# Expert tiles of 128 tokens, two per step with weights of their own, in an attention and mixture-of-experts kernel

## The chip, the cores and the metric

The kernel runs on one core of one Trainium2 chip. The metric is the device time of one execution in microseconds (us). A core has five engines with instruction streams of their own: TensorE (PE in the profile, its weight loads PEld), VectorE (DVE), ScalarE (ACT), GpSimd (POOL) and SyncE (SP), which here only issues DMAs. They meet by semaphores.

## The reference

```python
x = layernorm(x + attention(x))          # x: 8 x 512 x 256, float32
x = layernorm(x + experts(x))
# attention: 16 heads of 16, linear: q = elu(x Wq + bq) + 1, k likewise,
#   out = (sigmoid(x Wg + bg) * (q (k^T v))) Wo + bo
# experts: 16, inner width 128; softmax gate, 2 of 4 groups, top 4 of 16
a = silu(x w1[e]) * (x w3[e])
y = sum over the 4 chosen e of c[e] * (a w2[e])
z = silu(x ws1) * (x ws3) @ ws2          # shared expert, inner width 256
return y + z
```

## The kernel before

A float32 product is made of three half-width ones: each operand is split into a high part (float16, `_hi`) and a rest (bfloat16, `_lo`), and `product` (L1147) multiplies hi by hi, hi by lo and lo by hi. All expert weights lie in SBUF in both parts (`we_hi`, `we_lo`, 18 chunks: 2 of the shared expert, 16 of the others).

Stage one: a loop over 8 batches of 512 tokens does the attention, the first layer norm, and the routing. `assign_slots` gives each token a row in the region of each of its 4 experts, and GpSimd scatters the rows by indirect DMAs into `expert_in` in DRAM (`dispatch`). The batches are in two waves of 4 (2048 tokens, 8192 rows). SyncE meanwhile writes zeros into the rows behind the regions (`fill_spare`, 16 DMAs of 512 KB) and behind each region's last row (`fill_end`, 256 KB each, 16 for each wave; the second wave's 16 are issued one per step between steps 24 and 40 of the first wave).

Between the stages VectorE makes the plan of the first wave, `plan_pairs` in 8 dependent parts, which ends in two small tables on one partition: `pair_chunk` (the expert of each pair) and `pair_row` (its first row). Its place in VectorE's stream is behind `apply_gate(NB - 1)` and ahead of `shared_hidden(0)` and `residual(NB - 1)`. The shared expert of batches 0 to 2 is worked there too.

Stage two, the experts' steps: 48 steps for each wave, 96 in all. A step is a pair of 128-row tiles, 256 rows of one expert: 8192 rows are 32 pairs and each of the 16 experts may leave one begun. For each step
- SyncE reads the row number from `pair_row` into a register (L327), waits until the ring buffer of 4 is free, issues one load of 256 KB (L330), and waits for and issues the store of an earlier result (L334);
- TensorE's sequencer transposes the rows of step g + 2 (4 float32 transposes, L1340), reads the expert of step g from `pair_chunk` into a register (`chunk_of`, L1345), does `up_pair` (4 calls of `product`, 12 matmuls of 256 columns, with the expert's weights as the stationary operand, L1149 to L1151), then `down_pair` of step g - 2 (6 matmuls, L1367 to L1373). The steps stand in a loop over 8 of them; the first two of each turn of the loop read the expert of step g - 2 once more;
- ScalarE and VectorE split the transposed rows (L617, L1025), do silu (L634), the product with the other half (L1036), its split (L642, L1044), and the copy of the result (L624).

VectorE also has one small part of a plan or a weight table in each step of the first wave, and in the second wave it adds the first wave's gathered results (`combine`, L1055) and normalizes batches that are done (`final_norm`, L1070). GpSimd scatters the second wave's rows during the first wave's steps and gathers the first wave's results during the second's, both paced by `h_ready`, which `up_pair` counts up. Behind the last step the shared expert of the later batches and the gathering of the second wave remain.

The order on every engine is written out by hand.

```python
            def chunk_of(g):
                return pe.value_load(pair_chunk[0:1, g, :], min_val=SHARED, max_val=NCH - 1)
```

## Time and profile before

| | us |
|---|---|
| median of 3 runs | 711.87 (711.7 to 711.9) |
| the profiled execution | 707.36 |
| its span, first to last instruction | 705.5 |
| of it, attention stage | 0 to 230 |
| between the stages | 230 to 270.5 |
| the 96 steps | 270.5 to 589 |
| behind the last step | 589 to 705.5 |

The profile is one execution. Time stands in us from the span's start, durations of single instructions in ns where it is said. PE's matmuls are pipelined, so a matmul's duration is longer than the distance to the next one; the distance between starts is what a matmul costs in a stream. A "q" behind an engine's name marks instructions that its sequencer does alone: register operations, loads of a register from SBUF (TENSOR_LOAD), waits and the issue of DMAs. They don't count as busy time of the engine. The weight loads and matmuls are issued by one sequencer, and its own instructions are listed under PEldq.

### The profile page before, as it was taken

The numbers are of one execution on the slowest core, as the hardware profiler recorded it, in microseconds if no ns is written. First come the engines' busy times: TensorE is split into PE (matmuls) and PEld (weight loads), VectorE is DVE, ScalarE is ACT, GpSimd is POOL, SyncE is SP. The second block draws the span as 40 slices with busy tenths as digits, with TensorE's granted clock in tenths as the row PEclk, the third lists the DMA queues.
The fourth block names the chain that finished last, engine by engine and source line by source line (L and its number), as shares of the span: only waits on it lengthen the run. The fifth ranks groups of instructions, "written<-read, shape, count | busy, mean of one in ns | idle before, by whom it ended". The sixth has DMA issues, their size and how long they took to land.

```text
span 705.5 us, 13461 instructions
## 1 busy us (share of the span) xinstructions
PE 527.1 (75%) x3532; PEld 357.0 (51%) x3555; DVE 427.4 (61%) x1200; ACT 300.1 (43%) x659; POOL 290.1 (41%) x334
## 2 busy tenths in 40 slices
PE   1899887889897688789786688798888779665400
PEld 1355443555544357567574566576667566421300
DVE  2447783776864866666554444377757556652784
ACT  2536653436524343555454555356546445110100
POOL 1000126456446402454444200644446251777574
PEclk9999997899999899999999999899999989977755
DMA  7022428295451303767767766687787753333332
GB/s 202 13 75 76 156 90 284 82 304 209 177 185 68 103 18 106 239 204 230 232 228 259 238 223 216 180 235 233 211 261 231 223 181 134 105 120 89 94 114 99
DMA packets 64091, 118.63 MB, mean 168 GB/s; under 512 B 9760, under 2 KB 23088, under 8 KB 64048
## 3 DMA queue, kind: packets, MB, share of 16 engines
q1 hardware_dynamic: 51216, 84.55, 37.1%
q0 software_dynamic: 12288, 33.57, 15.1%
q8 instruction: 19, 0.31, 0.2%
q14 instruction: 24, 0.20, 0.1%
q10 hardware_dynamic: 544, 0.00, 0.0%
HBM read 55.17 MB, written 62.91 MB: 167 GB/s over the span
## 4 chain that ended last, share of the span: by engine, by line
PE 36%; DVE 19%; issue 15%; SPq 9%; another core or an unknown queue 6%; ACT 6%; DMA 5%; POOL 4%; ACTq 0%; DVEq 0%; POOLq 0%
PE t L1340 4%; PE h_even L1149 4%; PE h_even L1151 4%; PE h_odd L1149 3%; PE h_even L1150 3%; PE h_odd L1151 3%; PE h_odd L1150 3%; DVE x_all L1055 2%; SPq L327 2%; PE y L1186 2%; DMA kv<-expert_in 2%; SPq L330 1%; PE y L1373 1%; SPq L334 1%
## 5 line engine op out<-in xcount | busy, mean ns | idle before, releaser
L440 POOL DMA_INDIRECT expert_in<-x_all,slots x128 | 132.9, 1038 | 117.8 <-PE h_odd L1151 45.0
L452 POOL DMA_INDIRECT wa_stage<-expert_out,result_of x64 | 62.9, 983 | 35.3 <-issue 18.1
L1340 PE MATMUL t<-ident,kv 128*128 128x128 f32 x384 | 60.3, 280 | 19.4 <-DMA kv<-expert_in 15.0
L452 POOL DMA_INDIRECT q_fm<-expert_out,result_of x32 | 32.4, 1014 | 85.6 <-DMA expert_out<-q_exp 63.9
L426 POOL TENSOR_SCALAR neg_mean<-mv 128x4 f32<-128x4 f32 x16 | 4.6, 290 | 149.5 <-DVE mv L699 149.3
L1044 DVE TENSOR_TENSOR wa_lo<-bias_heads,wa_hi 128x256 bf16<-128x256 f32 x96 | 40.5, 422 | 41.3 <-ACT wa_hi L642 30.1
L1149 PE MATMUL h_even<-xsT_hi,we_hi 128*128 128x256 f16 x192 | 54.3, 283 | 10.7 <-issue 8.8
L1340 PEld LDWEIGHTS t<-ident,kv 128*128 128x128 f32 x384 | 45.3, 145 | 26.8 <-DMA kv<-expert_in 12.1
L1025 DVE TENSOR_TENSOR xsT_lo<-t,xsT_hi 128x512 bf16<-128x512 f32 x72 | 49.5, 688 | 11.6 <-ACT xsT_hi L617 5.9
L1150 PE MATMUL h_even<-xsT_lo,we_hi 128*128 128x256 bf16 x192 | 54.2, 282 | 2.5 <-issue 2.5
L1151 PE MATMUL h_even<-xsT_hi,we_lo 128*128 128x256 f16 x192 | 54.2, 282 | 1.4 <-issue 1.4
L617 ACT ACTIVATE xsT_hi<-t 128x512 f16<-128x512 f32 x72 | 42.0, 585 | 16.6 <-PE t L1340 12.8
L642 ACT ACTIVATE wa_hi<-bias_heads 128x256 f16<-128x256 f32 x96 | 39.7, 414 | 20.7 <-DVE bias_heads L1036 14.4
L1036 DVE TENSOR_TENSOR bias_heads<-h_odd,kv_heads 128x256 f32<-128x256 f32 x48 | 20.2, 420 | 41.8 <-ACT kv_heads L634 40.9
L1036 DVE TENSOR_TENSOR bias_heads<-h_even,kv_heads 128x256 f32<-128x256 f32 x48 | 20.1, 419 | 34.4 <-ACT kv_heads L634 30.9
L634 ACT ACTIVATE kv_heads<-h_odd 128x256 f32<-128x256 f32 x48 | 18.3, 381 | 52.8 <-remote 25.0
L1186 PE MATMUL y<-wo_sb,gated 128*128 128x256 f32 x128 | 33.3, 419 | 9.3 <-DVE gated L686 9.3
L452 POOL DMA_INDIRECT gate<-expert_out,result_of x32 | 30.5, 954 | 19.4 <-PE h_even L1151 10.0
L529 ACT ACTIVATE kv<-h_even 128x256 f32<-128x256 f32 x32 | 12.3, 386 | 58.3 <-PE h_even L1151 52.4
L634 ACT ACTIVATE kv_heads<-h_even 128x256 f32<-128x256 f32 x48 | 18.2, 380 | 43.8 <-PE h_even L1151 17.4
L1367 PE MATMUL y<-we_hi,wa_hi 128*128 x96 | 26.8, 279 | 12.6 <-issue 10.7
L624 ACT ACTIVATE k_exp<-y 128x512 f32<-128x512 f32 x48 | 28.7, 598 | 15.9 <-PE y L1373 14.3
(222 smaller groups left out, 1530.0 us busy)
## 6 DMA issues: line engine op xcount, KB each, us to landing
kv<-expert_in SPq DMA_DIRECT2D x96, 256.0 KB
expert_out<-k_exp SPq DMA_DIRECT2D x48, 256.0 KB
expert_out<-q_exp SPq DMA_DIRECT2D x48, 256.0 KB
expert_in<-wa_stage SPq DMA_DIRECT2D x16, 512.0 KB
expert_in<-wa_stage SPq DMA_DIRECT2D x32, 256.0 KB
stage<-in_L_ffn_w SPq DMA_DIRECT2D x48, 128.0 KB
x_in<-in_L_attn_x SPq DMA_DIRECT2D x8, 512.0 KB
out<-gated SPq DMA_DIRECT2D x8, 512.0 KB
```

Source lines behind the costliest of these rows:

```text
L440: pool.indirect_dma_start(xs_dram[b // WB], bass.IndirectOffsetOnAxis(ap=slots[:, b, t, j:j + 1], axis=0), x_all[:, b, t, :], None).then_i ...
L452: pool.indirect_dma_start(y_got[i][:, j, :], None, ys_dram[w], bass.IndirectOffsetOnAxis(ap=result_of[:, b, t, j:j + 1], axis=0)).then_inc ...
L617: act.activation(xsT_hi[r][:, :, :], t_bank[r % 2][:, :].rearrange("p (c n) -> p c n", c=KC), ACT.Copy).then_inc(xst_hi_ready, 1)
L642: act.activation(aT_hi[r % 2][:, :], a_pair, ACT.Copy).then_inc(at_hi_ready, 1)
L1025: dve.tensor_tensor(xsT_lo[r][:, :, :], t_bank[r % 2][:, :].rearrange("p (c n) -> p c n", c=KC), xsT_hi[r][:, :, :], ALU.subtract).then_in ...
L1036: dve.tensor_tensor(a_pair, h_banks[r % 2][0][:, 2 * P:], s_pair, ALU.mult).then_inc(pair_a_ready, 1)
L1044: dve.tensor_tensor(aT_lo[r % 2][:, :], a_pair, aT_hi[r % 2][:, :], ALU.subtract).then_inc(at_lo_ready, 1)
L1149: pe.matmul(dst, sta_hi, mov_hi, start=start, stop=False)
L1150: pe.matmul(dst, sta_hi, mov_lo, start=False, stop=False)
L1151: return pe.matmul(dst, sta_lo, mov_hi, start=False, stop=stop)
L1186: last = pe.matmul(y_bank[h][:, (t % 2) * D:(t % 2 + 1) * D], gated[:, c, t * P:(t + 1) * P], wo_sb[:, c, :], start=c == 0, stop=c == KC - 1)
L1340: last = pe.transpose(t_bank[r % 2][:, c * 2 * P + i * P:c * 2 * P + (i + 1) * P], xs[r][:, i, c * P:(c + 1) * P], ident[:, :])
```

## The change

The unit becomes a tile of 128 rows of one expert, planned tile by tile: 64 full tiles and 16 that may be begun give 80 tiles for each wave. A step takes two tiles, number g and number g + 40, and so two experts: 40 steps for each wave, 80 in all. Each step now reads two row numbers and issues two loads (of 128 KB, into 64 partitions each) on SyncE, reads two experts on TensorE, and does `up_pair` as 8 calls of `product` with 128 columns each. The transposes write every other column, so that the rows of each tile stand together. `down_pair` has 6 matmuls as before, with two experts' weights as the moving operand.

With it go: a ninth part in the plan, which works on 80 tiles where it worked on 48 pairs; a fifth part in `place_results`; half of the zero rows (8 DMAs of 512 KB, and 128 KB for each region's end); the pace of GpSimd's scatters and gathers in terms of the new steps; the final norm of batches 0 to 2 moved from VectorE to ScalarE (`final_norm` there), with a wait of GpSimd for it; the loops over the second wave's steps on VectorE and ScalarE written out. The plan of the first wave stands in VectorE's stream behind `residual(NB - 1)` and ahead of `shared_hidden(1)`. `gw_sb` shares the memory of `k_exp`, and several small tables that of `stage`.

```diff
-PLAN_STEPS = 8
+PLAN_STEPS = 9
...
-    NPAIR = WT * TOP_K // 2 + E
+    NTILE = WT * TOP_K + E
+    NPAIR = NTILE // 2
     PAIR = 2 * P
-    MOST = WB * S // PAIR
-    REGION = (MOST + 1) * PAIR
-    SPARE = NPAIR - WT * TOP_K // 2
-    SLOTS = E * REGION + SPARE * PAIR
+    MOST = WT
+    REGION = (MOST + 1) * P
+    SPARE = NTILE - WT * TOP_K
+    SLOTS = E * REGION + SPARE * P
...
-    PLAN_GROUPS = 7
+    PLAN_GROUPS = 8
+    NORM_PAIR = 17
...
-    assert SPARE * PAIR == FILLS * FILL_ROWS and FILLS == 8
+    assert SPARE * P == FILLS * FILL_ROWS and FILLS == 4
...
             def rows_of(dram, row):
-                return dram[bass.ds(row, PAIR), :].rearrange("(p t) d -> p t d", p=P)
+                return dram[bass.ds(row, P), :].rearrange("(p t) d -> p t d", t=2)
...
-                for i in range(4 * (b - 2), 4 * (b - 1)):
+                for i in range(3 * (b - 2), min(3 * (b - 1), WAVES * FILLS)):
                     fill_spare(i)
...
             next_x(NB - 1)
-            for i in range(12, WAVES * FILLS):
-                fill_spare(i)
...
             def load_xs(w, p, r, first=False):
 
-                row = sp.value_load(pair_row[0:1, NPAIR * w + p, :], min_val=0, max_val=SLOTS - PAIR)
+                rows = [sp.value_load(tile_row[0:1, h, NPAIR * w + p, :], min_val=0, max_val=SLOTS - P) for h in range(2)]
                 if not first:
                     sp.wait_ge(xs_transposed, NPAIR * w + p - RING + 1)
-                sp.dma_start(xs[r][:, :, :], rows_of(xs_dram[w], row)).then_inc(xs_loaded[r], 16)
+                for h in range(2):
+                    sp.dma_start(xs[r][h * P // 2:(h + 1) * P // 2, :, :],
+                                 rows_of(xs_dram[w], rows[h])).then_inc(xs_loaded[r], 16)
...
                 if 0 < k < WT:
-                    pool.wait_ge(h_ready, NPAIR + (3 * k if k < WT - TT else 3 * WT - 13 + 2 * (k - WT + TT)))
+                    pool.wait_ge(h_ready, NPAIR + 9 * k // 4)
...
                 if i > 0:
-                    pool.wait_ge(h_ready, 5 * i // 2)
+                    pool.wait_ge(h_ready, 2 * i)
...
-                        if b > 0 and t == (1 if w == 0 else TT - 1):
+                        if b > 0 and t == (2 if w == 0 else TT - 1):
+                            if 1 < b <= EARLY + 1:
+                                pool.wait_ge(out_ready, b - 1)
                             rstd_of(NB + b - 1)
...
+            for p in range(NPAIR):
+                pair(NPAIR + p, p % RING, GROUPS_OF_PAIRS + p // RING, p < NPAIR - 2)
+                b, t = (p - NORM_PAIR) // 9, (p - NORM_PAIR) % 9
+                if 0 <= b < EARLY and t < TT:
+                    final_norm(b, t)
...
             apply_gate(NB - 1, True)
-            for part in range(PLAN_STEPS):
-                plan_pairs(0, part)
...
             shared_hidden(0)
             residual(NB - 1, True)
+            for part in range(PLAN_STEPS):
+                plan_tiles(0, part)
             shared_hidden(1)
...
-                pe.wait_ge(xs_loaded[r], 16 * use)
+                pe.wait_ge(xs_loaded[r], 32 * use)
                 for c in range(KC):
+                    turned = t_bank[r % 2][:, c * PAIR:(c + 1) * PAIR].rearrange("p (k t) -> p k t", t=2)
                     for i in range(2):
-                        last = pe.transpose(t_bank[r % 2][:, c * 2 * P + i * P:c * 2 * P + (i + 1) * P],
-                                            xs[r][:, i, c * P:(c + 1) * P], ident[:, :])
+                        last = pe.transpose(turned[:, :, i], xs[r][:, i, c * P:(c + 1) * P], ident[:, :])
...
-            def chunk_of(g):
-                return pe.value_load(pair_chunk[0:1, g, :], min_val=SHARED, max_val=NCH - 1)
-
-            def up_pair(g, r, chunk):
+            def chunks_of(g):
+                return [pe.value_load(tile_chunk[0:1, h, g, :], min_val=SHARED, max_val=NCH - 1) for h in range(2)]
+
+            def up_pair(g, r, chunks):
...
-                for k in range(2):
-                    for c in range(KC):
-                        cols = slice((c * 2 + k) * INTER, (c * 2 + k + 1) * INTER)
-                        last = product(h_banks[r % 2][0][:, k * PAIR:(k + 1) * PAIR],
-                                       we_hi[:, chunk, cols], we_lo[:, chunk, cols],
-                                       xsT_hi[r][:, c, :], xsT_lo[r][:, c, :], c == 0, c == KC - 1)
+                for h, chunk in enumerate(chunks):
+                    tok = slice(h * P, (h + 1) * P)
+                    for k in range(2):
+                        for c in range(KC):
+                            cols = slice((c * 2 + k) * INTER, (c * 2 + k + 1) * INTER)
+                            last = product(h_banks[r % 2][0][:, k * PAIR + h * P:k * PAIR + (h + 1) * P],
+                                           we_hi[:, chunk, cols], we_lo[:, chunk, cols],
+                                           xsT_hi[r][:, c, tok], xsT_lo[r][:, c, tok], c == 0, c == KC - 1)
...
-                w2_hi, w2_lo = we_hi[:, chunk, W13:], we_lo[:, chunk, W13:]
...
+                for h, chunk in enumerate(chunks):
+                    last = product(y_bank[r % 2][:, h * D:(h + 1) * D],
+                                   aT_hi[r % 2][:, h * P:(h + 1) * P], aT_lo[r % 2][:, h * P:(h + 1) * P],
+                                   we_hi[:, chunk, W13:], we_lo[:, chunk, W13:], True, True)
```

## Rows read from the trace of the kernel before

**Rows 1.** Part 1 of the page: busy us, share of the span, instructions.

```profile
PE 527.1 (75%) x3532; PEld 357.0 (51%) x3555; DVE 427.4 (61%) x1200; ACT 300.1 (43%) x659; POOL 290.1 (41%) x334
```

**Rows 2.** Busy time by stretch: PE, PEld, DVE, ACT, POOL, clock, DMA share, GB/s.

```profile
270.50:589.00 318.50, 259.76 (x2089) 205.90 (x2090) 187.28 (x468) 165.16 (x378) 127.34 (x136) 0.96 0.69 219
...
370.00:390.00 20.00, 13.66 (x112) 10.38 (x110) 8.75 (x18) 8.99 (x21) 8.16 (x8) 1.00 0.78 254
...
110.00:120.00 10.00, 7.90 (x54) 3.61 (x54) 1.05 (x3) 2.73 (x4) 6.76 (x7) 0.99 1.01 366
```

**Rows 3.** Line 1149, 268 to 590: ns min/median/max, first to last start.

```profile
L1149 PE MATMUL h_even<-xsT_hi,we_hi x192: 269/273/421, 270.6 to 585.9; 128*128 128x256 f16 x192
...
L1149 PE MATMUL h_odd<-wa_hi,we_hi x96: 272/273/421, 277.8 to 587.8; 128*128 128x256 f16 x96
```

**Rows 4.** Timeline of PE, a step at full pace: start, us, instruction.

```profile
467.27 0.28 PE L1149 MATMUL h_even<-xsT_hi,we_hi 128*128 128x256 f16 x1
467.38 0.27 PE L1150 MATMUL h_even<-xsT_lo,we_hi 128*128 128x256 bf16 x1
...
469.68 0.27 PE L1149 MATMUL h_odd<-wa_hi,we_hi 128*128 128x256 f16 x1
```

**Rows 5.** TensorE's sequencer in one step, 469.45 to 471.78, by line.

```profile
L1149 PEldq FUSED_REGOPS  x4: 46/46/46, 469.5 to 470.2; - x4
...
L1151 PEldq ALU_OP  x4: 32/32/32, 469.6 to 470.3; - x4
...
L1364 PEldq EVENT_SEMAPHORE  x1: 51/51/51, 470.4 to 470.4; - x1
...
L1345 PEldq FUSED_REGOPS  x2: 42/96/151, 471.0 to 471.5; - x2
L1345 PEldq TENSOR_LOAD <-pair_chunk x1: 306/306/306, 471.1 to 471.1; - x1
L1345 PEldq SEQ_ASSERT  x1: 18/18/18, 471.7 to 471.7; - x1
```

**Rows 6.** The same view of line 1345 over all steps.

```profile
L1345 PEldq TENSOR_LOAD <-pair_chunk x118: 10/311/1293, 269.6 to 585.1; - x118
```

**Rows 7.** Timeline of weight loads, a step that begins on an idle PE.

```profile
388.69 0.10 PEld L1151 LDWEIGHTS h_even<-xsT_hi,we_lo 128*128 x1
388.84 0.10 PEld L1149 LDWEIGHTS h_even<-xsT_hi,we_hi 128*128 x1
```

**Rows 8.** Timeline of PE: matmuls of 32 columns, each with a weight load.

```profile
251.16 0.18 PE L1211 MATMUL t<-gwT_both,xT_hi 128*128 128x32 f16 x1
...
251.21 0.18 PE L1211 MATMUL t<-gwT_both,xT_hi 128*128 128x32 f16 x1
```

**Rows 9.** Waits of PE, 270 to 590: us in total, times, longest.

```profile
PE t L1340 <- DMA kv<-expert_in: 15.0, 11, 3.8
```

**Rows 10.** Timeline of weight loads in a starved stretch.

```profile
450.80 0.10 PEld L1369 LDWEIGHTS y<-we_lo,wa_hi 128*128 128x128 f16 x1 [0.61 <-issue]
```

**Rows 11.** Timeline of PE behind that stretch.

```profile
453.67 0.42 PE L1149 MATMUL h_even<-xsT_hi,we_hi 128*128 128x256 f16 x1
453.88 0.42 PE L1150 MATMUL h_even<-xsT_lo,we_hi 128*128 128x256 bf16 x1
```

**Rows 12.** SyncE's loads between 360.1 and 422: count, first to last issue.

```profile
L330 SPq DMA_DIRECT2D kv<-expert_in x17: 3/359/615, 360.9 to 421.4; - x17
```

**Rows 13.** All waits of SyncE in that stretch.

```profile
SPq L371 <- DMA expert_in<-wa_stage: 1.2, 1, 1.2
```

**Rows 14.** Timeline of DVE, the plan and the last residual.

```profile
232.15 0.99 DVE L844 TENSOR_TENSOR stage<-plan_sb,pairs_end 1x768 f32<-1x768 f32 x1
...
238.18 1.28 DVE L718 TENSOR_TENSOR x_all<-y,x_all 128x512 f32<-128x512 f32 x2
```

**Rows 15.** Timeline of ACT: the last batch's first norm.

```profile
243.37 2.07 ACT L510 ACTIVATE x_all<-x_all,shift,rstd 128x256 f32<-128x256 f32 x4 [0.82 <-POOL shift L431]
```

**Rows 16.** Timeline of SyncE: four fills of the attention stage.

```profile
108.05 3.12 SPq L292 DMA_DIRECT2D expert_in<-wa_stage  x4
```

More of the change, by code:

```diff
@@ L364, in _ @@
             sp.wait_ge(fill_rows_ready, 2)
[L365 to L367 removed]
+            with sp.Fori(2, (last - 1) // 2) as q2:
+                group(0, 2 * q2 + 1, fill=E + 2 * RING * (q2 - 2))
+                group(0, 2 * q2 + 2, fill=E + 2 * RING * (q2 - 2) + RING)
             sp.wait_ge(rows_ready, 2)
@@ L1026, in xst_lo, with pair @@
                                   xsT_hi[r][:, :, :], ALU.subtract).then_inc(xst_lo_ready, 1)
-            def pair(g, r, ahead=True, add=None, norm=None, whole=True, part=None):
+            def pair(g, r, ahead=True, add=(), part=None):
                 if ahead:
@@ L1037, in pair @@
                 if add:
-                    combine(0, *add[0], whole)
-                if norm is not None:
-                    final_norm(norm, r)
+                    combine(0, *add[0], add[0][0] < EARLY)
                 if part:
@@ L1073, in final_norm, with group @@
                     last.then_inc(out_ready, 1)
-            def group(q, b=None, tiles=(), norm=None, whole=True, parts=(), last=False):
+            def group(q, parts=()):
                 for r in range(RING):
-                    add = [(b, i // TOP_K, i % TOP_K) for i in tiles[r]] if tiles else None
-                    pair(RING * q + r, r, not (last and r >= 2), add, norm, whole,
-                         parts[r] if r < len(parts) else None)
-            q1 = GROUPS_OF_PAIRS
+                    pair(RING * q + r, r, part=parts[r] if r < len(parts) else None)
             xst_lo(0, 0)
```

151 lines of the change are left out of this document (74 added, 77 removed).

## The prediction

> **What bounds the kernel now.** I began with the page's first part [rows 1]: PE is busy for three quarters of the span, more than any other engine, but its busy time counts overlapping matmuls and is no proof of a bound. The busy times by stretch [rows 2] put 318.5 of the 705.5 us into the experts' steps, with the TensorE clock at 0.96, PE at 260 us, VectorE at 187 and ScalarE at 165. The change alters this stage most, so the rest is read there. The first and the last matmuls of line 1149 [rows 3] stand 317 us apart, so a step takes 317 / 95.5 = 3.32 us on average. The timeline of PE shows what a step costs when nothing is late [rows 4]: matmuls of 256 columns start 0.11 us apart, and the next step's first matmul starts 469.68 - 467.27 = 2.41 us later. Between them lie 12 matmuls of `up_pair`, 6 of `down_pair` and 4 transposes, 22 x 0.11. Of 3.32 us, then, 0.91 are stalls.
>
> The reader should next look at TensorE's sequencer, which no busy time shows. One step of it stands in [rows 5]. The four address computations of line 1149 run from 469.5 to 470.2 and the next wait (L1364) is at 470.4: about 0.95 us for `up_pair`, or 0.24 us for each `product` (one FUSED_REGOPS for the high weights' address, one ALU_OP for the low ones', six instructions for the array). `down_pair` and the transposes follow until 471.0: 0.55 us. Reading the expert into a register takes from 471.0 to the end of the view, where the next `up_pair` begins: 0.8 us (register operation, TENSOR_LOAD 0.31, register operation 0.15, assert, and the gaps between them). Together 2.3 us, just under the array's 2.41. The sequencer is hidden today by 0.1 us a step. That this rate is its own and not the array's is seen where a step begins on an idle PE [rows 7]: the first weight load behind an address computation comes 0.15 us after the one before it, though nothing is queued, where the others keep 0.11. TENSOR_LOAD has a median of 0.31 us over 118 loads and a longest of 1.29 [rows 6]; 118 is 96 steps and 22 repeats at the loop's turns.
>
> **The change, part by part: the steps.** It removes 16 of 96 steps. It adds to each of the remaining 80 the following.
>
> The array's work: 24 matmuls of 128 columns for 12 of 256. No f16 matmul of 128 columns is in the trace. The nearest rows are 256 columns at 0.11 [rows 4] and 32 columns at 0.025 (two starts in 0.05 us, [rows 8]); half of the first is 0.055, the second plus 96 columns at (0.11 - 0.025) / 224 each is 0.061. So 24 take 1.3 to 1.5 us where 12 took 1.32: next to nothing, and the array's floor is 2.4 to 2.6 us. The weight loads follow at 32 columns without a bubble, so doubling them costs no more. The strided writing of the transposes has no row; I take nothing for it, with 0 to 0.44 us a step (half speed) as bounds, all under the sequencer's time below.
>
> The Trainium skill, page "TensorE: Matmul & The Clock Gate", section "Back-to-back issue gap", speaks against the change here: it gives about 81 ns for a matmul of 128 columns in a stream with weight loads, so 24 would take 1.9 us, and the array's floor would be 3.0. The same section gives about 131 ns for 512 columns. By either figure the sum stays, since the array remains under the sequencer.
>
> The sequencer's work: `up_pair` has 8 products, each with addresses of its own, 8 x 0.24 = 1.9 us. `down_pair` has two experts' weights, one more pair of addresses, 0.2 us; with the transposes 0.75. Two reads of an expert, 2 x 0.8 = 1.6. Sum 4.25 us, against 2.3 now. Nothing hides it: the array needs 2.6. The repeats at the loop's turns are 9 x 2 x 2 = 36 reads, 36 x 0.8 / 80 = 0.35 us a step. Slow TENSOR_LOADs [rows 6]: between 0 and, if half of them took the double, 0.15 for each of 2.45 reads; I take 0.1 each, 0.25 a step. Together 4.85 us a step. 79.5 x 4.85 = 386 us.
>
> The Trainium skill, page "DMA: Bandwidth & Descriptors", section "Latency and other measured facts", gives a floor of about 600 ns for a register load of this kind. The trace has 0.31 [rows 6] and decides; by the page's figure 2.45 x 0.3 x 80 = 59 us would come on top.
>
> What of today's stalls stays? The 15.0 us in which PE waited for rows from DRAM [rows 9] go: the ring of four now gives 4 x 4.85 = 19 us for a load. Waits for ScalarE and VectorE go too, since both have less than 2.8 us of work in a step (today's 187 and 165 us over 96 steps are 2.0 and 1.7; the additions of the first wave's results crowd into 36 steps instead of 44, the final norm of three batches goes to ScalarE, 12 x 0.6). What does not go are stretches in which every engine's instructions come 0.7 us apart while GpSimd gathers [rows 10]: some 6 us there, and two or three like it. I keep 10 us, bounds 5 and 25, since there are more instructions to bring in. Experts' steps after: 396 us, against 317: **+79**.
>
> **SyncE's queue.** Each step reads two row numbers and issues three DMAs. The trace has that mix: between 360.1 and 422 each step also reads a fill row and issues a fill. There SyncE issued 17 loads in 60.5 us, 3.8 us a step [rows 12], and waited for nothing but 1.2 us at the end [rows 13], so it was its own bound. After the change 64 steps take 3.8 us of it, below 4.85. The 16 steps with a fill take a third read and a fourth DMA, 3.8 + 1.2 = 5.0: a little over. 16 x 0.15 = 2 us, inside the bounds.
>
> **The plan and the last residual.** The plan stands from 230.5 to 236.3, ahead of the residual at 238.2 [rows 14]. Four of its operations work on one partition over 768 elements, the first of them in 0.99 us [rows 14], of which some 0.95 are the elements; 1280 elements make them 1.6, so the plan grows from 5.8 to about 8.7 us with its ninth part. Moved behind the residual, it lets the residual start with the projection's end, some 4 us earlier, and GpSimd's square root after it is hidden. But `shared_hidden(1)` is now queued behind the plan on VectorE, ScalarE waits for it ahead of the last batch's first norm (it comes behind `shared(1)` in ScalarE's stream), and the transposes, the last routing and the first step wait for that norm. Residual's statistics done at about 237, plan to 245.7, product, split: the norm starts at 247 where it started at 243.4 [rows 15]: **+4**, bounds 0 and +7. The first loads need the plan only some 15 us later.
>
> **Fills.** Four fills are issued at 108 [rows 16], and DMA is full for the ten us behind them (share 1.01, 366 GB/s) while VectorE does 1 us of work [rows 2]. Each fill of 512 KB is 1.4 us at that rate. Half of 16 go; of these 8 perhaps three lie on the path of the attention stage: **-4**, bounds 0 and -10.
>
> **The tail** behind the last step keeps its gathers, its shared expert and its norms: 0, bounds -3 and +3. The moved final norm of three batches is beside the steps on both engines, and GpSimd's new wait for it asks for a norm three steps old: 0. The pace of scatters and gathers ends at the same share of a wave: 0.
>
> **Sum.** 707.4 + 79 + 4 - 4 = 786.4 for a profiled execution. The median of the runs is 4.5 us above the profiled one, so 790.9; I say 790.
>
> **The rivals.** (a) The clock falls. The array would work 2.6 of 4.85 us. Behind a stretch with few matmuls it ran at 1.2 GHz, and 256 columns took 0.21 us [rows 11]. Were that so through most of the steps, the array would need 22 x 0.21 / 2.41 of its pace, about 4.8 to 5.0 us, as much as the sequencer, and their delays would add: 0.5 us a step, +40, 830. For it: more idle time between matmuls. Against it: the matmuls stay spread evenly over the step, and the clock held at 1.00 in the 20 us from 370, where PE was busy for only 13.7 [rows 2].
>
> (b) SyncE's queue is the bound and not TensorE's sequencer, because a second read of an expert overlaps the first or addresses are computed once. Then 64 x 3.8 + 16 x 5.0 = 323, with 5 for starved stretches 328: +11, about 723.
>
> (c) On the other side, faster: the array's stream is the bound, with the sequencer hidden as today. Place: `up_pair`. Price: 80 steps of 2.6 + 0.91 us of today's stalls are 281, -36, about 676. It decides if a product's addresses and the two reads cost less than the array's 2.6 us together; at 3.95 us a step both kernels are equal (317 / 80), and above it the change loses. The reads alone are 1.6 and the eight products 1.9, so it needs both of my rates to be wrong, though [rows 5, 7] show them.
>
> **How the numbers follow.** Forecast (sequencer) 0.83, (a) 0.06, (b) 0.05, (c) 0.06. The forecast's own range: at 4.25 + 0.2 us a step with the favourable ends of the other parts, 354 + 5 - 317 - 10, so 744; at 5.2 with 25 of starved stretches 413 + 25 - 317, and +5 elsewhere, about 838. With (a) inside, the range 740 to 835 leaves out (b), (c) and the far ends. A difference of 0.2% is about what a measurement of this kernel can tell from none. Of (b) a fifth lies within it or below: faster 0.06, same 0.02, slower 0.92.
>
> **What would show it.** In the changed kernel's trace: some 4.85 us between the first matmuls of neighbouring steps; 8 address computations in a step, 0.24 us apart; 196 reads of an expert on TensorE; matmuls of 128 columns that start in threes with gaps between the threes; hardly any PE wait for DMA; the 80 steps over 380 to 410 us; fewer idle-free stretches of PE though it has more matmuls; the last first norm near 247. Wrong would be: steps under 3.9 us, address computations closer than 0.2, the clock at 0.5 over long stretches, or SyncE with no waits outside the fill steps.

## The result, and the profile after

The changed kernel takes 802.2 us (median of 4 runs, 797.3 to 811.7) against 711.8 for the kernel before beside it: a ratio of 1.126, with an interval of 1.120 to 1.131; the longest of the four runs counts as slow and is left out of the ratio. That is 90 us slower; 79 were forecast for a profiled execution and 78 for the median. The profiled execution has a span of 800.3 us, 94.8 more than that of the kernel before: that one's profiled execution was 4.5 us faster than its median, this one's was not. Its page begins, in the columns of [rows 1]:

```profile
PE 561.7 (70%) x4140; PEld 375.8 (47%) x4163; DVE 410.1 (51%) x1142; ACT 280.8 (35%) x607; POOL 290.6 (36%) x334
```

PE's busy share fell although it has 608 more instructions. The busy times by stretch, in the columns of [rows 2], are those between the stages, of the steps, of 20 us amid them, and behind the last step:

```profile
230.00:279.00 49.00, 32.52 (x208) 20.81 (x208) 36.94 (x133) 15.87 (x25) 10.73 (x13) 0.86 0.17 53
279.00:683.50 404.50, 294.02 (x2697) 223.46 (x2698) 167.48 (x406) 145.26 (x325) 126.32 (x136) 0.87 0.46 147
370.00:390.00 20.00, 14.49 (x136) 10.95 (x136) 7.74 (x30) 6.95 (x17) 7.69 (x8) 0.91 0.46 151
683.50:800.30 116.80, 51.05 (x249) 26.91 (x250) 66.33 (x170) 13.47 (x24) 71.71 (x84) 0.72 0.33 106
```

The first step begins 8.4 us later than it did (279.0 against 270.6), the tail is as long as before (116.8 against 116.5). The rest, 86 us, is in the steps, in which DMA moves less per us (147 GB/s against 219), VectorE and ScalarE have less to do, and the clock is at 0.87, where [rows 2] had 0.96. The first and the last matmul of the first line of `product` (it is L1161 now), as in [rows 3]:

```profile
L1161 PE MATMUL h_even<-xsT_hi,we_hi x320: 217/228/314, 279.0 to 678.5; 128*128 128x128 f16 x160
...
L1161 PE MATMUL h_odd<-wa_hi,we_hi x160: 219/227/314, 290.1 to 682.3; 128*128 128x128 f16 x160
```

From 279.0 to 682.3 are 403.3 us, where the kernel before took 317.2: **+86** of the 94.8 between the two traces. Over 79.5 steps that is 5.07 us a step. A step at full pace, from the timeline of PE (compare [rows 4]); the last line is the next step's first matmul:

```profile
453.76 0.23 PE L1161 MATMUL h_even<-xsT_hi,we_hi 128*128 128x128 f16 x1 [0.98 <-issue]
453.82 0.22 PE L1162 MATMUL h_even<-xsT_lo,we_hi 128*128 128x128 bf16 x1
453.88 0.22 PE L1163 MATMUL h_even<-xsT_hi,we_lo 128*128 128x128 f16 x1
454.00 0.23 PE L1161 MATMUL h_even<-xsT_hi,we_hi 128*128 128x128 f16 x1
...
455.82 0.28 PE L1161 MATMUL y<-we_hi,wa_hi 128*128 x1
...
456.49 0.60 PE L1353 MATMUL t<-ident,kv 128*128 128x128 f32 x4
458.06 0.23 PE L1161 MATMUL h_odd<-wa_hi,we_hi 128*128 128x128 f16 x1 [0.97 <-issue]
```

458.06 - 453.76 = 4.30 us. The matmuls come in threes, 0.06 apart, and the next three start 0.24 after the last three did: the third is followed by 0.12 and not 0.06, and in this gap the sequencer works out the next addresses. `up_pair` takes 2.06 us (eight times 0.24, and the way into `down_pair`), then `down_pair` and the transposes, and at the end the array stands empty for 0.97 us with "issue" as the reason: two reads of an expert. All waits of PE in the steps (us in total, times, longest) say the same, against [rows 9]:

```profile
PE h_even L1161 <- issue: 33.4, 33, 2.2
PE y L1161 <- issue: 26.8, 20, 2.6
PE h_odd L1161 <- issue: 20.1, 23, 1.7
...
PE t L1353 <- DMA kv<-expert_in: 2.3, 3, 0.8
```

The view names only idle times of some length; in it 80 us are PE's own sequencer ("issue"; what it does then is an inference here, tested below), and the wait for rows from DRAM is down from 15.0 to 2.3. What the other queue does is in the waits of SyncE, over all steps:

```profile
SPq L337 <- ACT q_exp L629: 33.7, 19, 3.8
SPq L337 <- ACT k_exp L629: 29.1, 15, 7.9
```

It waits for ScalarE's results for 63 of 404 us. In the 16 steps in which a fill is issued (375 to 463) it hardly waits (1.4 us in all between 370 and 470), and these take 5.44 us each, against 4.81 ahead of them.

### The profile page after: what moved, and what is told of

The parts are those of the page before. It is cut to its first block, busy times and chain, and to the rows that moved or that the text cites. A ratio compares the mean times of both kernels' runs of the same rounds, so it can differ in the third digit from the quotient of the medians.

```text
span 800.3 us, 15510 instructions
## 1 busy us (share of the span) xinstructions
PE 561.7 (70%) x4140; PEld 375.8 (47%) x4163; DVE 410.1 (51%) x1142; ACT 280.8 (35%) x607; POOL 290.6 (36%) x334
## 4 chain that ended last, share of the span: by engine, by line
PE 36%; issue 19%; DVE 17%; SPq 9%; another core or an unknown queue 8%; ACT 5%; POOL 3%; DMA 2%; ACTq 0%; DVEq 0%; POOLq 0%
PE h_even L1161 5%; PE h_odd L1161 4%; PE h_even L1163 4%; PE t L1353 3%; PE h_even L1162 3%; PE y L1161 3%; PE h_odd L1163 3%; SPq L328 3%; PE h_odd L1162 2%; DVE x_all L1079 2%; SPq L332 2%; PE y L1198 2%; PE y L1162 2%; PE y L1163 2%
## 5 line engine op out<-in xcount | busy, mean ns | idle before, releaser
L1161 PE MATMUL h_even<-xsT_hi,we_hi 128*128 128x128 f16 x320 | 78.7, 246 | 41.0 <-issue 33.4
L1161 PE MATMUL y<-we_hi,wa_hi 128*128 (+1 forms) x192 | 59.0, 308 | 39.4 <-issue 30.2
L1163 PE MATMUL h_even<-xsT_hi,we_lo 128*128 128x128 f16 x320 | 77.2, 242 | 1.2 <-issue 1.1
L1162 PE MATMUL h_even<-xsT_lo,we_hi 128*128 128x128 bf16 x320 | 77.2, 242 | 0.0
L1062 DVE TENSOR_TENSOR bias_heads<-h_even,kv_heads 128x256 f32<-128x256 f32 x40 | 17.0, 425 | 97.2 <-ACT kv_heads L649 96.2
L1161 PEld LDWEIGHTS h_even<-xsT_hi,we_hi 128*128 x320 | 33.5, 105 | 63.5 <-issue 51.0
L1162 PE MATMUL y<-we_lo,wa_hi 128*128 (+1 forms) x192 | 58.6, 305 | 4.8 <-issue 4.7
L1163 PE MATMUL y<-we_hi,wa_lo 128*128 (+1 forms) x192 | 58.4, 304 | 3.6 <-issue 3.6
L1062 DVE TENSOR_TENSOR bias_heads<-h_odd,kv_heads 128x256 f32<-128x256 f32 x40 | 17.0, 424 | 75.5 <-ACT kv_heads L649 73.1
L1161 PE MATMUL h_odd<-xsT_hi,we_hi 128*128 128x128 f16 x160 | 41.7, 264 | 15.0 <-issue 9.5
L1161 PE MATMUL h_odd<-wa_hi,we_hi 128*128 128x128 f16 x160 | 37.5, 235 | 16.9 <-issue 10.5
L1161 PEld LDWEIGHTS y<-we_hi,wa_hi 128*128 128x128 f16 x192 | 20.6, 107 | 56.1 <-issue 51.8
```

The source lines that it names most:

```text
L1062: dve.tensor_tensor(a_pair, h_banks[r % 2][0][:, 2 * P:], s_pair, ALU.mult).then_inc(pair_a_ready, 1)
L1161: pe.matmul(dst, sta_hi, mov_hi, start=start, stop=False)
L1162: pe.matmul(dst, sta_hi, mov_lo, start=False, stop=False)
L1163: return pe.matmul(dst, sta_lo, mov_hi, start=False, stop=stop)
```

## The experiments

Four theories are tried: (S) TensorE's sequencer sets the steps, by 0.24 us for each product with an address of its own and 0.8 us for each read of an expert; (Q) SyncE's queue sets them, rival (b); (A) the array sets them, as in rival (c), or dearer, by more time for a matmul of 128 columns, as in the section of the Trainium skill quoted against the change; (C) the lower clock makes most of the loss, rival (a). Three groups of kernels ran on three chips, on which the kernel before took 696, 647 and 709 us. So ratios and differences are compared within a group where that can be done. In the first group it can't wholly: the changed kernel itself was not run there, and its ratio to the kernel before was 1.126, 1.155 and 1.138 where it was. Mean steps are the distance of the first matmuls of the first and the last step by their number.

**First group: taking TensorE's costs away from the changed kernel.** One read for both tiles:

```diff
-                return [pe.value_load(tile_chunk[0:1, h, g, :], min_val=SHARED, max_val=NCH - 1) for h in range(2)]
+                return [pe.value_load(tile_chunk[0:1, 0, g, :], min_val=SHARED, max_val=NCH - 1)] * 2
```

> The changed kernel with one read of an expert per step in place of two: both tiles of a step are worked with the weights of the first tile's expert (the second tile's expert is left out, so the result for it is another). All address computations, matmuls, loads and stores stay. Theory S (TensorE's sequencer is the bound): the read takes 0.76 us, 98 of 196 go, so steps at full pace fall from 4.3 to 3.55 us; SyncE's queue, at 3.8 us a step with this mix of reads and DMAs, may then be what is left. Time 725 to 740 against 802. Theory A (the array is the bound, by 24 matmuls of 128 columns with their weight loads): no change, 802. Theory C (the clock, 0.87 against 0.92, made most of the loss): 795 to 802.

And both reads kept, but the weights of two fixed chunks used, so that no address is computed:

```diff
-                for h, chunk in enumerate(chunks):
+                for h, chunk in enumerate((SHARED, SHARED + 1)):
```

(the same in `down_pair`).

> The changed kernel in which both reads of a step stay, but the matmuls take the weights of two fixed experts, so that no address is computed from a register (the choice of the expert is left out). The same 34 matmuls with their weight loads per step. Theory S: 20 address computations of 0.09 us go, steps at full pace fall from 4.3 to some 2.5 us, so the array (2.6) and SyncE (3.8) are left: 690 to 725. Theory A: the array's work is the same, 802. It also shows the distance between matmuls of 128 columns when nothing holds them back: 0.057 by my estimate, 0.081 by the Trainium skill's page.

They took 752.4 and 749.4 us, 1.081 (1.065 to 1.098) and 1.077 (1.060 to 1.094) of the kernel before, where the changed kernel has 1.126 to 1.155: each gives back a third to a half of the loss. Both fell short of what S alone expected (725 to 740 and 690 to 725, against 802). PE's timeline of the second, in a step that nothing holds up:

```profile
291.44 0.23 PE L1161 MATMUL h_even<-xsT_hi,we_hi 128*128 128x128 f16 x1
291.50 0.22 PE L1162 MATMUL h_even<-xsT_lo,we_hi 128*128 128x128 bf16 x1
291.56 0.22 PE L1163 MATMUL h_even<-xsT_hi,we_lo 128*128 128x128 f16 x1
291.61 0.22 PE L1161 MATMUL h_even<-xsT_hi,we_hi 128*128 128x128 f16 x1
...
293.88 0.22 PE L1161 MATMUL h_odd<-wa_hi,we_hi 128*128 128x128 f16 x1
```

Without the addresses the matmuls stand 0.055 us apart with no gap behind the third, and the step takes 293.88 - 291.44 = 2.44 us with both reads in it. So the gap in the changed kernel is the address, and theory A falls: the array's floor did not move (2.41 before). The 81 ns that the Trainium skill's page "TensorE: Matmul & The Clock Gate", section "Back-to-back issue gap", gives for this case are 55 here, with a weight load for each matmul; the measurement decides.

But only five steps are that short; the mean is 4.36, and 4.44 with one read. What holds the others? In the kernel with one read, all waits of SyncE from 370 to 470, and below them PE's longest waits over the steps:

```profile
SPq L374 <- DMA expert_in<-wa_stage: 1.0, 1, 1.0
SPq L337 <- ACT q_exp L629: 0.2, 1, 0.2
```

```profile
PE t L1353 <- DMA kv<-expert_in: 53.5, 42, 2.7
```

Between 370 and 470 SyncE never rests, and over the steps PE now waits for rows in 42 places, 53.5 us in all. This edit takes more than a read from TensorE, as the third group shows: with one expert for both tiles the addresses are computed once as well. Yet the steps shorten by far less than that. As soon as TensorE's sequencer is relieved, SyncE's queue takes over. With the fixed addresses it does so in part: 25.1 us of waits for rows, beside over 60 us of "issue", since all the reads are still there. Q is not the bound of the changed kernel over most of its steps, but it is right behind.

**The same costs given to the kernel before.** Each read of an expert made twice, and `up_pair` in halves of 128 columns of the same expert:

```diff
             def chunk_of(g):
+                pe.value_load(pair_chunk[0:1, g, :], min_val=SHARED, max_val=NCH - 1)
                 return pe.value_load(pair_chunk[0:1, g, :], min_val=SHARED, max_val=NCH - 1)
```

> The kernel before with each read of an expert made twice (118 reads more), nothing else. Theory S: the sequencer's 2.3 us a step become 3.1 and the array's 2.41 no longer hide it. 118 x 0.76 = 90 us of sequencer time, of which 96 x 0.1 were free and part of today's stalls of 0.9 us a step is covered: plus 35 to 75, so 747 to 787. Theory A or C: the sequencer has room, 712 to 720.

```diff
-                for k in range(2):
-                    for c in range(KC):
...
-                                       xsT_hi[r][:, c, :], xsT_lo[r][:, c, :], c == 0, c == KC - 1)
+                for h in range(2):
+                    tok = slice(h * P, (h + 1) * P)
+                    for k in range(2):
+                        for c in range(KC):
...
+                                           xsT_hi[r][:, c, tok], xsT_lo[r][:, c, tok], c == 0, c == KC - 1)
```

> The kernel before with up_pair cut in halves of 128 columns, both with the same expert: 24 matmuls and 16 address computations per step for 12 and 8, one read, 96 steps, all rows and loads as before. Theory S: 0.95 us more in the sequencer, 3.25 us a step at full pace: plus 45 to 80, 757 to 792, and in the trace the pairs within a product 0.057 apart with a gap behind each third. Theory A by 0.081 a matmul: 24 of them take 1.94, 3.05 us a step, about the same time, but with even distances of 0.08. The two part in the distances. If neither holds (matmuls of 128 at 0.057 and addresses hidden): 712 to 720.

The second read made it 736.7 us, 1.059 (1.048 to 1.069): +41, as S says; a step of 3.65. The halves made it 725.4 us, 1.042 (1.035 to 1.050): +29 and a step of 3.52, less than the 45 to 80 expected. The expectation was wrong on what the build does: with the same expert in both halves the four pairs of addresses are computed once and kept for the second half (382 FUSED_REGOPS of this line in 95 steps, not 760). So the two prices stand side by side in one step. Its timeline, from its first matmul to the next step's:

```profile
418.19 0.23 PE L1149 MATMUL h_even<-xsT_hi,we_hi 128*128 128x128 f16 x1
418.43 0.23 PE L1149 MATMUL h_even<-xsT_hi,we_hi 128*128 128x128 f16 x1
...
419.26 0.22 PE L1149 MATMUL h_even<-xsT_hi,we_hi 128*128 128x128 f16 x1
419.43 0.22 PE L1149 MATMUL h_even<-xsT_hi,we_hi 128*128 128x128 f16 x1
...
420.93 0.23 PE L1149 MATMUL h_odd<-wa_hi,we_hi 128*128 128x128 f16 x1
```

A product takes 0.24 us in the first half, where its addresses are worked out, and 0.17 in the second, where they are not. The first half is thus bound by the sequencer, and the step takes 420.93 - 418.19 = 2.74 us instead of 2.41. Over 96 steps that is some 30 us, the +29 measured: twice as many matmuls of half the columns cost the array nothing more, but they are too short to hide an address of their own, as those of 256 columns (0.33 us for three) do.

**Second group: the plan's place, the fills, the repeats.** The changed kernel once more, and the same with the plan put back ahead of `shared_hidden(0)`:

> The changed kernel itself, beside the next three on the same chip, as their reference: 1.12 to 1.13 times the kernel before.

```diff
             apply_gate(NB - 1, True)
+            for part in range(PLAN_STEPS):
+                plan_tiles(0, part)
...
             residual(NB - 1, True)
-            for part in range(PLAN_STEPS):
-                plan_tiles(0, part)
```

> The changed kernel with the first wave's plan back ahead of shared_hidden(0) and the last residual. In the trace of the changed kernel the last batch's first norm starts 7.1 us later than in that of the kernel before, and VectorE stands idle for 4.1 us ahead of shared_hidden(0). Theory P (the plan's place costs the 7 us, since ahead of shared_hidden(0) it would lie in that idle time): the norm starts at 244 to 246 and the time falls by 5 to 7 us. Rival (as I predicted it, the residual starts earlier without the plan ahead of it, and the move costs little): 0 to 3 us. Second rival: the steps' start is bound by loads or the shared expert, and nothing comes of it at the end: 0.

The changed kernel took 748.7 us (748.2 to 748.8) beside 647.3, a ratio of 1.155 (1.147 to 1.163); with the plan ahead 746.2 (743.1 to 747.0). So its place costs 2.5 us, less than the 5 to 7 expected; the two kernels' runs don't overlap, but 0.3% is little for four runs each. VectorE's timeline, first of the changed kernel, then with the plan ahead; each ends with the first operation of the routing that stands behind the plan and the norm (that of the batch before the last):

```profile
220.84 0.69 DVE L1010 TENSOR_TENSOR x_in<-h_even,x_in 128x512 f32<-128x512 f32 x1 [1.91 <-ACT x_in L603]
...
222.84 1.48 DVE L736 TENSOR_TENSOR x_all<-y,x_all 128x512 f32<-128x512 f32 x2
...
226.09 0.39 DVE L845 TENSOR_TENSOR stage<-total,plan_sb 128x256 f32<-128x256 f32 x1
...
236.24 0.21 DVE L760 TENSOR_REDUCE r_sum<-r_exp 128x4 f32<-128x64 f32 x1
```

```profile
217.38 0.42 DVE L845 TENSOR_TENSOR stage<-total,plan_sb 128x256 f32<-128x256 f32 x1
...
225.56 0.67 DVE L1012 TENSOR_TENSOR x_in<-h_even,x_in 128x512 f32<-128x512 f32 x1
...
227.54 1.28 DVE L736 TENSOR_TENSOR x_all<-y,x_all 128x512 f32<-128x512 f32 x2
...
232.56 0.21 DVE L760 TENSOR_REDUCE r_sum<-r_exp 128x4 f32<-128x64 f32 x1
```

Ahead, the plan (8.2 us) begins at once and covers the 1.91 us for which VectorE otherwise waits in `shared_hidden(0)`. Behind, the residual does start earlier (222.84 against 227.54), but the wait is back and the plan comes on top, ahead of what the norm needs. The routing is 3.7 us earlier with the plan ahead, of which 1.5 were there already (the last head mask stands at 213.88 and 212.41 in the two traces): 2.2 are left, near the 2.5 of the times.

This group also answers theory C. On this chip the clock was at 0.96 over the changed kernel's steps, and the loss is 101 us, more than the 90 of the first comparison, with the clock at 0.87. A step takes 4.70 us, where the next kernel, whose steps are those of the kernel before, has 2.87.

The kernel before with half of its fills (spare rows of both waves are left unwritten):

```diff
-    FILLED = 16 * (FILLS + E)
+    FILLED = 16 * (FILLS // 2 + E)
...
-                for i in range(4 * (b - 2), 4 * (b - 1)):
+                for i in ((0, 1, 2), (3, 8, 9), (10, 11))[b - 2]:
```

> The kernel before with 8 of its 16 fills of 512 KB (3, 3 and 2 in the three batches, as in the change; the other spare rows are left unwritten, so results of unused rows differ). As predicted: -4 us, bounds 0 and -10. Rival, from the trace of the changed kernel, where the attention stage with half of the fills was no shorter (last batch's head mask at 226.3 against 224.3): 0, the stalls of that stage have another cause.

643.9 us, 0.993 (0.990 to 0.996): 3.4 us less by the medians and 4.4 by the ratio, about the forecast's 4. It comes from the attention stage: the same operation of its last batch, in this kernel and then in the next one, which keeps all fills, is 3.9 us earlier:

```profile
209.08 0.69 DVE L917 SCALAR_TENSOR_TENSOR q_fm<-q_exp,q_fm 128x512 f32<-128x512 f32 x1 [4.94 <-ACT q_exp L555]
```

```profile
212.97 0.69 DVE L919 SCALAR_TENSOR_TENSOR q_fm<-q_exp,q_fm 128x512 f32<-128x512 f32 x1 [4.94 <-ACT q_exp L557]
```

The gain is shown for this chip alone. In the first and third groups the last head mask stands at 223.9 to 227.5 in the kernels with half of the fills, and at 225.6 to 226.1 in those with all: single executions, but no gain of 4 us is in them.

The kernel before with TensorE's steps written out, so that no expert is read twice:

```diff
-            with pe.Fori(1, GROUPS_OF_PAIRS // 2) as q2:
-                two_groups(2 * q2)
+            for q2 in range(1, GROUPS_OF_PAIRS // 2):
+                chunks = two_groups(2 * q2, before=chunks)
```

> The kernel before with TensorE's steps written out in place of the loops over 8 steps: the 22 repeated reads of an expert at the loop's turns go (the registers are kept), and the table's addresses are constants, 0.1 us less per read. Theory S, which by now says that the sequencer bounds the kernel before as well: 22 x 0.76 + 96 x 0.1 = 26 us of its 2.5 us a step go, of which half to all shows, until the array's 2.41 takes over: -8 to -20 us. Rival (the array and late data bound the kernel before, and the sequencer is beside them): 0 to -3 us. If written-out code comes late from DRAM: slower.

637.0 us, 0.982 (0.975 to 0.989): 10 to 12 us less than the 647.3 beside it, and faster than both kernels. 22 reads of 0.8 us are 17.6, and the table's addresses, now constants, save some 0.1 us for each of 96 more reads by the expectation, 26 in all; less than half of it shows. The sequencer is thus part of the bound of the kernel before too.

**Third group: which queue, and how much.** The changed kernel, the same with TensorE's steps written out (the edit above), one read on TensorE and on SyncE, and the kernel before with SyncE's work of the changed one:

> The changed kernel once more, as the base for its variants on this chip. Theory S (TensorE's sequencer bounds the steps, 4.3 us at full pace): steps of 4.7 to 5.1 us on average, and a time 1.12 to 1.16 of the kernel before.

> The changed kernel with TensorE's steps written out instead of looped, so that the 36 repeated reads of an expert go (160 instead of 196) and with them the turns of the loop. Theory S with 0.8 us for each read: 36 x 0.8 = 29 us less, a step of 4.35 instead of 4.7. Theory Q (SyncE's queue, at 4.2 us a step, is so near behind that it takes over): the steps cannot get under 4.2 to 4.4 us, 5.1 in the 16 with a fill, so 15 to 25 us less. A theory by which the sequencer is not the bound: no difference beyond 5 us.

```diff
-                rows = [sp.value_load(tile_row[0:1, h, NPAIR * w + p, :], min_val=0, max_val=SLOTS - P) for h in range(2)]
+                rows = [sp.value_load(tile_row[0:1, 0, NPAIR * w + p, :], min_val=0, max_val=SLOTS - P)] * 2
```

> The changed kernel with one read a step on TensorE and one on SyncE: both tiles take the expert and the row number of the first, so the second tile's results are left out; the two loads and everything else stay. The kernel with one read on TensorE alone had steps of 4.44 us, 5.18 in the fill steps, with SyncE waiting for nothing. Theory Q: SyncE's second read of about 0.8 us was the bound there; without it the steps fall by 0.5 to 0.8 us, to 3.6 to 3.9, where TensorE's sequencer (4.3 - 0.8 = 3.5) is the bound again, and the kernel takes 60 to 80 us less than the changed one. If TensorE's sequencer or the clock bounded that kernel and not SyncE: the steps stay at 4.4, and the time is only 40 to 55 us less than the changed one's.

```diff
-                row = sp.value_load(pair_row[0:1, NPAIR * w + p, :], min_val=0, max_val=SLOTS - PAIR)
+                rows = [sp.value_load(pair_row[0:1, NPAIR * w + p, :], min_val=0, max_val=SLOTS - PAIR) for h in range(2)]
...
-                sp.dma_start(xs[r][:, :, :], rows_of(xs_dram[w], row)).then_inc(xs_loaded[r], 16)
+                for h in range(2):
+                    sp.dma_start(xs[r][h * P // 2:(h + 1) * P // 2, :, :],
+                                 half_rows_of(xs_dram[w], rows[h])).then_inc(xs_loaded[r], 16)
```

> The kernel before with the changed kernel's work on SyncE alone: two reads of a row number and two loads of 128 KB a step (both take the first 128 rows of the pair, so half of the rows are left out), TensorE's work as it is. Rival (b) of the prediction: SyncE's queue alone sets 3.8 us a step, 5.0 with a fill: 80 x 3.8 + 16 x 5.0 = 384 us of steps against 317, some 60 us slower. By the rate seen since (SyncE without waits at 4.2 to 4.4 us a step, 5.1 with a fill): 80 to 110 us slower. If SyncE's queue were no bound at all: within 5 us of the kernel before.

| third group | us | ratio to before (interval) | us a step |
|---|---|---|---|
| kernel before | 708.9 | | |
| changed | 806.3 | 1.138 (1.128 to 1.147) | 5.11 |
| changed, steps written out | 774.4 | 1.097 (1.088 to 1.106) | 4.74 |
| changed, one read on both queues | 711.9 | 1.004 (1.001 to 1.007) | 3.91 |
| before, SyncE's work of the changed | 789.9 | 1.117 (1.109 to 1.125) | 4.17 |

The 36 repeated reads, with the turns of the loop, are worth 32 us (29 by S; the 15 to 25 that theory Q expected fall short). With one read on each queue the change costs nothing that matters, 94 us less than the changed kernel and 3 above the kernel before: more than the 60 to 80 that Q expected. The register operations of TensorE on the first line of `product`, in the changed kernel and in this one:

```profile
L1161 PEldq FUSED_REGOPS  x800: 3/46/707, 279.3 to 687.5; - x160
```

```profile
L1161 PEldq FUSED_REGOPS  x400: 3/46/653, 283.2 to 596.0; - x134
```

10 in a step and 5: with one expert a step, its addresses are computed once for both tiles. So the loss is the second expert: its reads on both queues and its addresses. The smaller matmuls, the two smaller loads and the fuller plan, which this kernel has too, are together no dearer than the 16 steps that the change saves; that they cost nothing is not shown, since a step of 3.91 us is longer than one of the kernel before (3.3 in its first trace). The last kernel leaves TensorE's work alone and is still 81 us slower. Its waits of SyncE and the first of PE, over the steps:

```profile
SPq L339 <- ACT q_exp L629: 3.8, 2, 1.9
SPq L339 <- ACT k_exp L629: 2.2, 4, 1.0
```

```profile
PE t L1345 <- DMA kv<-expert_in: 65.1, 54, 4.0
```

SyncE's queue is a bound by itself: 4.17 us a step, 5.1 in the 16 steps in which a fill is issued (386 to 464) and 3.98 in the others. The forecast had 5.0 and 3.8. (In the kernel before the fills go out with the loads of steps 32 to 47; the 24 to 40 named ahead of the prediction are those of the changed kernel.) Over 96 steps that is +81; the changed kernel has 80, and 64 x 3.98 + 16 x 5.1 = 336 would be some 19 us above the 317 of the kernel before, where rival (b) said 11.

## Why the prediction was right, and where it was not

The result is within the range, and the forecast's main mechanism, TensorE's sequencer, is the one that the runs show. That the time for a step came so near is in part luck: a term for slow loads is hardly there, and waits that were to go fill its place. By its steps:

*The sequencer's sum.* The working gave 4.25 us for a step; the timeline has 4.30. The prices hold singly: the 0.24 us of a product are the distance of the threes, and vanish with the addresses (second kernel); the reads are 0.97 us of an empty array for two, since some 0.5 of their 1.5 us passes while the array still has work queued. The repeats were put at 0.35 us a step and measure 5.11 - 4.74 = 0.37. The slow TENSOR_LOADs were put at 0.25 us a step and are hardly there: 196 of them have a median of 0.302 us and a mean of 0.335, which makes 0.08 a step. On the chip of the second group the changed kernel has 4.70 us a step, with the clock at 0.96; 4.25 + 0.35 + 0.08 are 4.68.

*The steps as a whole: +79 forecast, +86 measured, and 5.07 us a step instead of 4.98 (396 / 79.5).* The steps without a fill take (403.3 - 16 x 5.44) / 63.5 = 4.98 us, the number forecast, but with other parts in it. The 0.25 for slow loads is hardly there. In its place stand waits for VectorE, which the forecast let go: `up_pair` waits for `bias_heads` (L1062) for 19.0 us in this trace (11.4 and 7.6, 0.24 a step), where the kernel before had 2.9. In the third group it is 19.1 again, and 2.7 on the second group's chip, where the steps take 4.70. And there are late steps at the lower clock (below). Those with a fill were to take 5.0 by SyncE's queue, and took 5.44: 16 x 0.46 = 7 us, which is the difference. Part of it is that issuing a fill of 128 KB from 64 partitions takes SyncE longer than the fill of 256 KB from 128 that the forecast was read from (ns, min/median/max; the changed kernel on the chip of the second group, then the last kernel of the third group, which kept the old fills):

```profile
L300 SPq DMA_DIRECT2D expert_in<-wa_stage x12: 527/528/545, 355.5 to 413.4; - x12
```

```profile
L300 SPq DMA_DIRECT2D expert_in<-wa_stage x11: 345/351/352, 386.2 to 440.2; - x11
```

The loads have the same surcharge (below). The rest goes with the disturbed stretches of the last section: on the second group's chip, which has hardly any, the fill steps take 4.91.

Inside the 4.98 rival (a) came true in part: the clock was at 0.87 over the steps. In 44 of 79 steps of this trace the granted clock was full, and they take 4.70 us on average; the other 35 take 5.6. The clock stood at its lower level, 1.2 GHz, for 99 us in 20 stretches. How much of the 0.9 us is the clock can't be told from these runs, since several of the stretches follow a long wait of PE (it waited 2.58 us up to 317.5, and the clock fell at 319.4), in steps that are late anyway. The kernel before had 8 such steps of 95.

*The array* was put at 1.3 to 1.5 us for 24 matmuls; 0.055 each are 1.32. The strided writing of the transposes, taken at nothing, has no cost in the 2.44 us step.

*The waits for DMA* went from 15.0 to 2.3, as forecast. 4 x 4.85 us for a load are enough.

*SyncE.* The rate of 3.8 us was read from one stretch of the kernel before [rows 12], whose mix of two reads and three DMAs was right. The error is that, per load, it took the issue time of 256 KB: a load of 128 KB into 64 partitions is dearer to issue than one of 256 KB into 128. The issue instructions over the steps of the changed kernel (ns, min/median/max), and below them those of the kernel before:

```profile
L332 SPq DMA_DIRECT2D kv<-expert_in x148: 3/479/1350, 279.7 to 662.6; - x148
```

```profile
L330 SPq DMA_DIRECT2D kv<-expert_in x90: 3/349/726, 270.5 to 570.3; - x90
```

It is dearer by 0.13 us. Two of them are 0.26, more than the 0.2 us by which SyncE's steps without a fill exceed the 3.8. That makes both queues bounds within some 0.6 us of each other (4.0 and 4.6), which the prediction did not weigh; it took rival (b) as a case apart from the forecast (0.05), where it is the next limit under it.

*The plan and the residual: +4 forecast; the norm is 7.1 us later.* ScalarE's timeline, against [rows 15]:

```profile
249.93 0.63 ACT L607 ACTIVATE a_hi<-x_in 128x512 f16<-128x512 f32 x1 [12.10 <-DVE x_in L1010]
250.47 1.08 ACT L515 ACTIVATE x_all<-x_all,shift,rstd 128x256 f32<-128x256 f32 x2
```

That is just outside the bounds of 0 and +7. VectorE's timeline, against [rows 14]:

```profile
235.99 0.69 DVE L1010 TENSOR_TENSOR x_in<-h_even,x_in 128x512 f32<-128x512 f32 x1 [4.12 <-remote]
...
237.98 1.28 DVE L736 TENSOR_TENSOR x_all<-y,x_all 128x512 f32<-128x512 f32 x2
...
241.04 0.39 DVE L845 TENSOR_TENSOR stage<-total,plan_sb 128x256 f32<-128x256 f32 x1
```

The step that failed in this trace is "it lets the residual start with the projection's end, some 4 us earlier". The residual starts at 237.98 where it started at 238.18, and its statistics are done at 241.1, not at 237; from there on the working holds (plan to 249.3, norm 1.2 us later). Two things took the 4 us. The last head mask was 2.0 us later already (226.31 against 224.32), of which no run shows the cause. And `shared_hidden(0)`, which stands ahead of the residual, now waits in the open for what the old plan had covered: 4.12 us, first for ScalarE's silu, which ends at 234.28, and then for 1.7 us more that the trace puts down to nothing it shows ("remote"). On the second group's chip these 1.7 us are missing (the wait is 1.91, and ends with the silu). There the step came true: counted from the last head mask, the statistics are done 3.5 us earlier than in the kernel before with half of its fills, and the norm starts 3.8 us later, against the +4 forecast. In the first pair of traces it is 5.1 later by that count, and 2.0 for the mask make the 7.1.

*The fills: -4.* The pair of traces shows no such gain (the head mask is 2.0 later), and neither do the first and third groups; the run made for it on the second group's chip does (3.4 to 4.4). So the start of the steps, put at +4 - 4 = 0, moved by 8.4 us, and this is over half of the 15.7 us by which the profiled execution (802.1 against 786.4) missed the sum. *The tail: 0*, and it is 0.3.

*The rivals.* (c), the array, is out: addresses and reads cost more than 2.6 us, at the rates that the forecast used. (a) is not the cause of the loss (second group), but a part of the late steps. (c)'s point of equality, 3.95 us a step, is borne out by a run: the changed kernel with one read on each queue has 3.91 us a step and takes 711.9 us against 708.9. (b) is not the bound of most steps, but of those with a fill. The sign "SyncE with no waits outside the fill steps" did not appear: it waited for 63 us.

## What to carry to other kernels

Cost a change of tiling on the sequencers first: registers read from memory, addresses computed and DMAs issued, for each queue, since they show in no busy time. Where one queue is just hidden, list the next ones with their own sums, since here two queues at 4.0 and 4.6 us nearly made one bound, and relieving one of them gives back only the difference. Ask of a shorter matmul whether it is still long enough to hide its own address. And before moving work from in front of a wait, look at whether the wait is its cover: the idle time shows in the trace only once the work is gone.

## What the runs showed of the hardware beyond that

Issuing a load of 128 KB into 64 partitions takes SyncE 0.48 us, a load of 256 KB into 128 partitions 0.35; writing 128 KB of zeros by 64 partitions takes 0.53 to issue, 256 KB by 128 takes 0.35. The smaller transfer is the dearer one on its queue, and its place behind another DMA is not the reason: the first of the two loads, which like the old one follows a store, takes 0.50.

Three chips ran the same kernel in 709, 696 and 647 us, and the difference shows in part in the instruction streams. SyncE's instructions for the loads over the steps of the changed kernel, on the chip of the second group and on that of the third:

```profile
L332 SPq FUSED_REGOPS  x148: 37/43/47, 264.6 to 617.1; - x148
```

```profile
L332 SPq FUSED_REGOPS  x148: 3/43/833, 280.0 to 665.4; - x148
```

The medians are the same, but on the chip of the third group such an operation can take 0.8 us, and some of the next ones nothing. In these steps 69 neighbouring instructions of SyncE start 0.66 to 0.76 us apart there (49 us in all), and 6 on the chip of the second group. In the changed kernel's trace of the first section they are 65, and 63 of them lie between 1 us ahead of and 2 us behind the start of one of GpSimd's indirect DMAs, where only half of the time of the steps lies. These are stretches like that of [rows 10], which the prediction put at 10 us. Why one chip has them and the other hardly any stays open; no run was made for it. The steps before measure 3.32 us with them and the changed ones 5.1; on the chip with hardly any the same steps take 2.87 and 4.70. The loss by the change is larger there (1.155), since the kernel before gains at least as much in us (62 against 58 from the third group's chip) and is the shorter one.
